# Attention output of a transformer block on one core: heads' sums through DRAM without transposes, divided as rows

## The reference

```
Q, K, V = heads(x @ Wq), heads(x @ Wk), heads(x @ Wv)      # (b, head, s, 8)
weights = softmax(mask(Q K^T / sqrt(8)))
attn = (weights @ V).reshape(b, s, 128)                    # no transpose back
x = layernorm(x + attn @ Wo + bo)
```

## Time and profile before

| | |
|---|---|
| Median of 3 runs | 1116.17 us (1111.87 to 1117.45) |
| Profiled execution: time, span | 1118.13 us, 1116.4 us |
| Mean granted clock of PE, share of full | 0.964 |
| Busy: PE, DVE, POOL, ACT | 87%, 74%, 61%, 60% |
| One period of the attention loop | 43.8 us |

### The profile page before, as it was taken

How to read it: one execution, slowest core, us unless ns; L and a number is a source line. 1 busy time by engine, 2 the same in 40 slices (tenths; PEclk the granted TensorE clock), 3 DMA queues, 4 the chain that set the end, 5 groups by cost and what they waited for, 6 DMA issues and landing times.

```text
span 1116.4 us, 29852 instructions
## 1 busy us (share of the span) xinstructions
PE 966.8 (87%) x9185; PEld 640.2 (57%) x9185; DVE 830.4 (74%) x2262; ACT 665.9 (60%) x1338; POOL 683.8 (61%) x1063
## 2 busy tenths in 40 slices
PE   3789999999999989999999999879899889998750
PEld 1344454454545545544455455349899879997740
DVE  4777878888888898898888888974455455467744
ACT  1256657666666676676666766646475745556552
POOL 7022445775766766756657667666668546557874
PEclk9699999999999999999999999979899999999985
DMA  7523133143242342432432423343222223265515
GB/s 168 186 74 115 57 96 121 50 138 102 65 137 91 87 128 64 121 122 51 138 101 66 134 74 98 117 139 89 71 73 71 78 67 87 71 200 183 166 54 169
DMA packets 134569, 117.75 MB, mean 105 GB/s; under 512 B 56218, under 2 KB 99777, under 8 KB 134240
## 3 DMA queue, kind: packets, MB, share of 16 engines
q1 hardware_dynamic: 121808, 96.37, 29.7%
q0 software_dynamic: 8704, 17.06, 4.5%
q10 hardware_dynamic: 3904, 2.43, 0.9%
HBM read 65.26 MB, written 53.81 MB: 107 GB/s over the span
## 4 chain that ended last, share of the span: by engine, by line
PE 43%; DVE 18%; POOL 11%; issue 10%; ACT 7%; DMA 6%; SPq 4%; ACTq 1%; DVEq 0%; POOLq 0%
PE ring L1132 9%; PE ring L1148 9%; DVE negmax L1192 8%; PE ps_v L1072 5%; PE ring L1009 4%; PE ring L1040 4%; ACT probs L730 3%; POOL probs L598 2%; PE ring L1055 2%; SPq L397 2%; POOL rows_d L610 2%; PE ps_m L937 2%; POOL y_d L640 2%; DMA rows<-att_d 2%; PE ps_m L902 2%
## 5 line engine op out<-in xcount | busy, mean ns | idle before, releaser
L730 ACT ACTIVATE probs<-ring 128x768 f32<-128x768 f32 (+1 forms) x384 | 337.3, 883 | 213.5 <-PE ring L1009 212.5
L1192 DVE TENSOR_REDUCE negmax<-ring 128x2 f32<-128x1024 f32 (+3 forms) x512 | 409.3, 812 | 67.5 <-PE ring L1055 63.8
L598 POOL TENSOR_SCALAR_AFFINE_SELECT probs<-probs 128x512 f32<-128x512 f32 x256 | 163.6, 639 | 247.5 <-ACT probs L730 245.4
L840 ACT ACTIVATE vpad<-ring,b_s 128x128 f32<-128x128 f32 x576 | 165.0, 371 | 107.8 <-PE ring L1132 105.9
L640 POOL DMA_INDIRECT y_d<-vpad,xs x144 | 146.1, 1015 | 102.3 <-DVE vpad L1496 75.4
L1009 PE MATMUL ring<-qarea,kside 64*128 64x512 f32 (+3 forms) x1024 | 178.6, 387 | 24.0 <-DVE negmax L1192 18.0
L1040 PE MATMUL ring<-kside,qarea 64*128 64x256 f32 (+2 forms) x1024 | 166.5, 363 | 28.8 <-ACT probs L730 15.1
L1009 PEld LDWEIGHTS ring<-qarea,kside 64*128 64x128 f32 x1024 | 87.3, 187 | 179.3 <-issue 118.8
L1072 PE MATMUL ps_v<-probs,vpad 128*32 128x512 f32 (+3 forms) x2048 | 180.4, 448 | 1.8 <-POOL probs L598 1.8
L1148 PE MATMUL ring<-qarea,vpad 128*128 x1152 | 157.5, 280 | 20.1 <-ACT vpad L840 20.0
L1132 PE MATMUL ring<-vpad,w_t 128*128 128x128 f32 x1152 | 157.1, 280 | 8.8 <-issue 8.6
(11 more groups left out here) (178 smaller groups left out, 1162.8 us busy)
## 6 DMA issues: line engine op xcount, KB each, us to landing
qk_d<-qarea SPq DMA_DIRECT2D x62, 256.0 KB, 2.6
kside<-qk_d SPq DMA_DIRECT2D x96, 128.0 KB, 3.0
qarea<-qk_d SPq DMA_DIRECT2D x90, 128.0 KB
xs<-rows_d SPq DMA_DIRECT2D x144, 66.0 KB, 1.9
probs<-y_d SPq DMA_DIRECT2D x16, 512.0 KB
xin<-L_attn_x SPq DMA_DIRECT2D x16, 256.0 KB, 3.0
att_d<-attt SPq DMA_DIRECT2D x128, 32.0 KB
rows<-att_d SPq DMA_DIRECT2D x16, 256.0 KB
```

What stands on the lines that cost most here:

```text
L598: pool.affine_select(out=diag, in_=diag, pattern=[[0, 4], [1, P]], compare_op=ALU.is_ge, fill=0.0, base=0, channel_multiplier=-1).then_inc ...
L730: nc.scalar.activation(of_unit(h // 2, part), ring[:, 2 * part % 3, :, (0, P, P)[part]:S], ACT.Exp, scale=SCALE).then_inc(sem("exp_done"), 1)
L840: ins = nc.scalar.activation(ht[:, n % 4, c, :], ps_a[:, n % 4, c * P:(c + 1) * P], ACT.Gelu_apprx_tanh, bias=b1_s[:, bass.ds(e, 1), c:c + ...
L1192: ins = nc.vector.tensor_reduce(negmax[:, n // 6 % 2, qb, s:s + 2], ring[:, (2 * n + 1) % 3, :, c0:c0 + nk], AX.X, ALU.max, negate=True)
```

## The change

The divide moves from the transposed layout to the loaded rows. ACT copies `ps_v` into `ucp`, now two halves, with the 16 rows of each group brought together by a strided write. Each half is stored at once from that layout, values and sums, by four transfers of 64 KB (in runs of 128 bytes), so eight transfers and 512 KB a block. Four loads of 128 KB (in runs of 512 bytes) bring the values as `rows16` and the sums, in the same layout, as `sums16`. DVE takes the reciprocal of all of `sums16` (128x512) at half step 21 and multiplies `rows16` by it at 22; stage wo waits for that product. The stages uT and aT, `urec`, `att` and `attt` go. The rows come in another order of channels, so Wo's rows are loaded permuted, by eight transfers instead of one, and Wq, Wk and Wv are loaded plainly, one transfer each. ACT's copy of V moves from the middle of step 4 to the start of step 5. On SP, `store_attention` of k = 1 and `load_attention` of block i - 1 now stand ahead of `store_x2`, and `store_attention` of k = 0 of block i behind it; in the tail they stand at steps 5 and 7, and `store_x2` at 6.

```
-    att_d = nc.dram_tensor("att_d", (16, HD, NH, S // 16), F32, kind="Internal").ap()
+    att_d = nc.dram_tensor("att_d", (2, 2, 2 * HD, 16, NH // 2, S // 16), F32, kind="Internal").ap()
...
-                5: ("mT", 0, 2), 6: ("uT", -1, 1), 7: ("aT", -1, 0), 9: ("mT", 0, 3), 10: ("nT", -2, 0),
-                12: ("wo", -1, 0), 13: ("mT", 1, 0), 14: ("uT", 0, 0)}
+                5: ("mT", 0, 2), 9: ("mT", 0, 3), 10: ("nT", -2, 0),
+                12: ("wo", -1, 0), 13: ("mT", 1, 0)}
...
             if i.loop or i.value < NB:
+                store_attention(sp, prev, 1)
+                load_attention(sp, prev)
                 store_x2(sp, prev.plus(-1))
-                store_attention(sp, prev)
-                load_attention(sp, prev)
+                store_attention(sp, i, 0)
...
+        def store_attention(sp, b, k):
             if not b.exists(NB):
                 return
+            need(sp, sem("u_copied"), 2, b, k + 1, sem("sp_passed"))
+            if k == 0:
+                need(sp, sem("rows16_in"), 64, b, -64, sem("sp_passed"))
+            for j in range(GH):
+                sp.dma_start(att_d[b.parity, :, :, :, GH * k + j].rearrange("a c r o -> (a c) r o"),
+                             ucp[32 * j:32 * j + 32, k].rearrange("p (r o) -> p r o", r=16)).then_inc(
+                    sem(f"att_stored{k}"), 16)
...
+            for k in range(2):
+                need(sp, sem(f"att_stored{k}"), 16 * GH, b, 16 * GH, sem("sp_passed"))
             need(sp, ready("wo"), 1, b, 0, sem("sp_passed"))
-            sp.dma_start(rows16[:, :], att_d.rearrange("r d h o -> (r d) (h o)")).then_inc(sem("rows16_in"), 16)
+            for what, t in ((0, rows16), (1, sums16)):
+                for a in range(2):
+                    sp.dma_start(t[:, :].rearrange("p (k a m) -> p a k m", k=2, a=2)[:, a],
+                                 att_d[b.parity, a, HD * what:HD * what + HD].rearrange(
+                                     "c r (k j) o -> (c r) k (j o)", k=2)).then_inc(sem("rows16_in"), 16)
...
-            load_heads(sp, wk_s, wk, "wk_in")
-            load_heads(sp, wv_s, wv, "wv_in")
-            sp.dma_start(wo_s[:], wo).then_inc(sem("weights_in"), 16)
+            sp.dma_start(wk_s[:], wk).then_inc(sem("wk_in"), 16)
+            sp.dma_start(wv_s[:], wv).then_inc(sem("wv_in"), 16)
+            for d in range(HD):
+                sp.dma_start(wo_s[16 * d:16 * d + 16, :], wo[d:D:HD, :]).then_inc(sem("weights_in"), 16)
...
-            load_heads(act, wq_s, wq, "wq_in")
+            act.dma_start(wq_s[:], wq).then_inc(sem("wq_in"), 16)
...
                 need(act, sem("pv_done"), 4, b, 2 * k + 2)
-                need(act, ready("uT"), 2, b, k)
-                nc.scalar.activation(ucp[:], ps_v[:], ACT.Copy).then_inc(sem("u_copied"), 1)
+                need(act, sem(f"att_stored{k}"), 16 * GH, b, 0)
+                nc.scalar.activation(ucp[:, k].rearrange("p (r o) -> p o r", r=16),
+                                     ps_v[:].rearrange("p (o r) -> p o r", r=16), ACT.Copy).then_inc(
+                    sem("u_copied"), 1)
...
             def st_wo(b, place):
-                need(pe, sem("rows16_in"), 16, b, 16)
+                need(pe, sem("rows_ready"), 1, b, 1)
...
+            def divide(b, part):
+                if part == 0:
+                    need(dve, sem("rows16_in"), 64, b, 64)
+                    nc.vector.reciprocal(sums16[:], sums16[:]).then_inc(sem("recip"), 1)
                 else:
+                    need(dve, sem("recip"), 1, b, 1)
+                    nc.vector.tensor_tensor(rows16[:], rows16[:], sums16[:], ALU.mult).then_inc(sem("rows_ready"), 1)
...
-                            if at == 13:
-                                divide(prev, 1, False)
-                                divide(prev, 1, True)
+                            if at in (21, 22):
+                                divide(prev, at - 21)
...
-                        if i.exists(NB) and at == 29:
-                            divide(i, 0, False)
-                            divide(i, 0, True)
```

More of the change, by code:

```diff
@@ L89, in build_program @@
     RING = 12
-    WEIGHTS = 6
+    WEIGHTS = 5 + 8
     assert (S, D, NH, QB, FC, E) == (512, 128, 16, 4, 4, 8) and NB % 2 == 0
@@ L128, in build_program @@
         xt = sb("xt", [P, S])
[L129 to L132, removed]
+        ucp = sb("ucp", [P, 2, S])
         rows16 = sb("rows16", [P, S])
+        sums16 = sb("sums16", [P, S])
         ysum = sb("ysum", [P, QB, D])
@@ L309, in place_max @@
                 sem("max_placed"), 16)
[L311 to L317, removed]
         def store_side(sp, b, side, what, hl):
@@ L487, in body @@
                     for h in range(NH):
+                        if h == 6:
+                            store_x2(sp, i.plus(-2))
                         if h == 5:
[L489 to L492, removed]
+                            store_attention(sp, i.plus(-1), 1)
+                        if h == 7:
                             load_attention(sp, i.plus(-1))
@@ L732, in body @@
                                                      ACT.Exp, scale=SCALE).then_inc(sem("exp_done"), 1)
+                        if h == 5 and u == 0 and nxt.exists(NB):
+                            copy_v(act, nxt)
                         if u != 1 and h in (0, 1) and rb.exists(NB):
@@ L816, in middle @@
                     nc.scalar.activation(rv[:, 4], rv[:, 3], ACT.Exp).then_inc(sem("gate_exp"), 1)
-                if prev.exists(NB):
-                    if h == 7:
-                        need(act, ready("aT"), 1, prev, 1)
-                        need(act, sem("att_stored"), 16 * HD, prev, 0)
-                        nc.scalar.activation(attt[:].rearrange("p (r o) -> p o r", r=16),
-                                             ps_m[:].rearrange("p (o r) -> p o r", r=16),
-                                             ACT.Copy).then_inc(freed("aT"), 1)
             def hidden(n):
@@ L883, in misc @@
                         break
-                if not i.loop and i.value >= NB and (name, i.value) in (("uT", NB), ("nT", NB + 1)):
+                if not i.loop and i.value >= NB and (name, i.value) in (("nT", NB), ("nT", NB + 1)):
                     pe.wait_ge(sem("route"), ROUTE * (i.value - 3) + 14)
@@ L910, in st_v @@
                 if not b.loop and b.value == 0:
-                    pe.wait_ge(sem("wv_in"), 16 * 4)
+                    pe.wait_ge(sem("wv_in"), 16)
                 for q in range(QB):
@@ L922, in st_mT @@
                 return ins
-            def st_uT(b, k):
-                need(pe, sem("u_copied"), 2, b, k + 1)
-                return tr(lambda q: ucp[:, q * P:(q + 1) * P])
-            def st_aT(b, place):
-                need(pe, freed("uT"), 2, b, 2)
-                return tr(lambda q: att[:, q, :])
             def st_wo(b, place):
-                need(pe, sem("rows16_in"), 16, b, 16)
+                need(pe, sem("rows_ready"), 1, b, 1)
                 if not b.loop and b.value == 0:
@@ L1226, in low_part @@
                                         ALU.subtract).then_inc(freed(stage), 1)
-            def divide(b, k, second):
-                of = ps_m[:].rearrange("p (q a c) -> p q a c", q=QB, c=16)
-                if not second:
-                    need(dve, ready("uT"), 2, b, k + 1)
-                    nc.vector.reciprocal(urec[:], of[:, :, :, 8]).then_inc(sem("recip"), 1)
-                else:
-                    need(dve, sem("recip"), 2, b, k + 1)
-                    need(dve, ready("aT"), 1, b, 0)
-                    nc.vector.tensor_tensor(att[:, :, 64 * k:64 * k + 64].rearrange("p q (a d) -> p q a d", d=HD),
-                                            of[:, :, :, 0:HD], along(urec[:], HD), ALU.mult).then_inc(freed("uT"), 1)
+            def divide(b, part):
+                if part == 0:
+                    need(dve, sem("rows16_in"), 64, b, 64)
+                    nc.vector.reciprocal(sums16[:], sums16[:]).then_inc(sem("recip"), 1)
+                else:
+                    need(dve, sem("recip"), 1, b, 1)
+                    nc.vector.tensor_tensor(rows16[:], rows16[:], sums16[:], ALU.mult).then_inc(sem("rows_ready"), 1)
             def statistics(b, which, src):
```

20 lines of the change are left out of this document (5 added, 15 removed).

## The result

The changed kernel takes 1191.6 us at the median (1190.7 to 1203.2, 4 runs), the kernel before beside it 1116.8 us: a ratio of 1.070 (95% interval 1.065 to 1.074). 1142 us was forecast, 1116 to 1156 as the range: the sign was right, the loss three times as large. The profiled execution has a span of 1189.9 us, 73.5 more than before, and a mean clock of 0.920 instead of 0.964.

What follows compares the result with a forecast made beforehand. PE and DVE, both nearly full and feeding each other through the PSUM ring, were taken as the bound. +33.6 stall, -4.4, -0.8 start, -3.8 + 1 tail gave +25.6 us on 1116.2: 1142 us, range 1116 to 1156.

Steps and rivals of the forecast that it cites:

- What goes out: Work removed per block: twelve PE transposes (1.9 us), two reciprocals and two products of DVE (1.53 us), one strided ACT copy (1.09 us).
- What comes in: Work added per block: DVE reciprocal of 128x512 at 3.1 us, product at 0.69 us; strided ACT copies taken as zero.
- rival 1: The dense reciprocal is fast (0.69 us), so nothing is paid at the wo product: about 1107 us; chance 0.14.
- Steps 10 to 12, where it is paid: The new DVE work makes PE wait ahead of the product with wo: +2.4 us in each of 14 blocks, +33.6 us.
- Rival 2: The stall is partly given back, half of 33.6 us regained before step 4: 1125 us; chance 0.20.
- Steps 6 and 7: Removed divide lets L1288 slip in ahead of POOL's product: -0.4 us a block in 11 blocks; bounds 0 and 1.1.
- Step 14: Transposes and divide removed there gain zero, as PE still waits for DVE or ACT; 0.7 a block otherwise.
- SP's queue: Stores and loads of rows stay hidden: rows in at 461.7 to 466.1, against 466.07 when DVE wants them.
- rival 3: The rows come late and the reciprocal starts up to 1.5 us later, +21 us: 1163 us; chance 0.08.
- Start and tail: Shorter wait for wk at the start -0.8 us; earlier rows in the tail -3.8, slow reciprocal +1.
- the slip: At step 6, L1288 gets in 0.12 us earlier, before POOL's product, shortening its long wait: -4.4 us over 11 blocks.

Runs made afterwards that it cites:

- e15: The kernel before, with ScalarE's two copies of the sums written strided; everything else stays: ratio 1.0004.
- e5: The kernel before, with one reciprocal of a 128x512 tile of ones added to DVE at half step 21 of each block, for which nobody waits: ratio 1.011.
- e12: The kernel before, with the four-element instruction L1288 alone moved one half step earlier: ratio 1.0037.
- e13: The changed kernel, with SP waiting for the placements of Q to land before it issues the stores of the sums of k = 1: ratio 1.079.
- e8: The kernel before, with the load of the attention rows in the tail put at step 9 instead of 11: ratio 1.0002.
- e3: The changed kernel, with twelve transposes that nothing reads put on PE just ahead of its wait for the divided rows in step 12: 1171.3 us, ratio 1.050.
- e2: The changed kernel, with three groups of four transposes of other data put back on PE at steps 6, 7 and 14: 1202.1 us, ratio 1.074.

## Why the prediction was wrong

- **What goes out** held in its prices and brought almost nothing: of the 1.2 us by which PE is earlier at step 8, 0.6 became the wait for Q in the block shown, and a second half at the full clock is only 0.2 us shorter (21.08 for 21.30).
- **What comes in.** The reciprocal took 3.34 us, 6.2 ns an element by the forecast's own fixed part, where 3.1 and 5.8 were forecast: right in kind, rival 1 is out. The Trainium skill's repeat count of 8 (VectorE: DVE Perf Modes, "First, the fixed hardware budget") made an estimated 4.4 us, which the trace does not bear out. Product 0.68 for 0.69, strided copies 1.07 for 1.09, at no cost (e15).
- **Steps 10 to 12, where it is paid** is the step that failed, by what it left out. The direct stall was forecast at 2.4 us and measured 2.3. But the step ended with PE taking up its work at full speed. In 12 of 14 blocks the clock fell to half between 0.3 us before and 2.8 us after the end of the wait, and stayed there for 3 to 10 us. That cost 31 us in the first halves; another 12 went with the half clock of the second, whose cause is open. No term, bound or rival held this. The earlier trace rows showed a clock of 1.00 and no idle of such length on PE. Yet the kernel before has such a half too, at 158 us: PE waits 0.87 us for the rows' DMA in it, and with 3.4 us at half clock it lasts 24.9 us, where the two beside it last 22.1 and 22.9.
- **Rival 2** went the wrong way: nothing was given back. e5 shows when DVE's time is partly absorbed (0.9 of 3.3 us paid): when PE does not stand waiting for its end.
- **Steps 6 and 7.** The -4.4 us were not earned. L1268, the former L1288, starts a little earlier against POOL's mask and product, ahead of both, and is still held to the product's end (L667, 499.59 + 1.27). DVE, then POOL, in one iteration of after:

```profile
498.85 2.05 DVE L1268 TENSOR_SCALAR rv<-rv 128x4 f32<-128x4 f32 x1
```

```profile
498.99 0.64 POOL L599 TENSOR_SCALAR_AFFINE_SELECT probs<-probs 128x512 f32<-128x512 f32 x1
499.59 1.27 POOL L667 TENSOR_TENSOR xc<-xc,gam_b 128x512 f32<-128x512 f32 x1
```

  e12 shows that even all of it would have brought nothing: the term was mis-sized in its bounds as well.
- **Step 14** and **SP's queue** held; rival 3 is out, but 2 to 3 us later would have been too late in five blocks (e13).
- **Start and tail.** The first K product starts at 5.85 instead of 6.56 us (0.7 of 0.8). From the last copy of the sums (at 824.5, before at 747.0) to the end of the span 365.4 us pass instead of 369.4: -4.0. The -2.8 that was summed had +1 for the last attention block in it; that block alone lost 6.5 us. e8 leaves open what part of the -4.0 is the earlier load.

With the missing 44 us of clock and without the 4.4 of the slip, the forecast's sum of 25.6 would have been 74. That it meets the 73.5 is partly luck: the stall was summed some 2 to 5 us too high, the last block some 6 too low.

## What to carry to other kernels

A wait put in front of the matrix engine in a loop that keeps it 94% busy is not priced by its length: look at the granted clock behind waits that the kernel already has, and add the time at half clock times what a microsecond of it costs in that loop (0.40 here). Work taken off an engine counts only if the next thing it waits for is not due at the same point, and a long instruction of the engine that feeds it costs least in parts, in steps where nobody stands waiting for its end (1.016 against 1.070).

## What was unexpected in the hardware

- Twelve PE transposes added in a wait made the kernel 20 us faster (e3).
- PE's clock fell behind the wait in 12 of 14 blocks of the changed kernel. There the wait was 2.28 to 3.15 us; in the two others it was 1.69 (the half from 509.76) and 2.24 us. Length alone does not decide: e2 has a fall behind 1.49 us, and e3 falls in four of 14 blocks behind the same 0.73 us.
- DVE's reciprocal of data in SBUF costs 6.2 ns an element at 512 elements (3343 ns) and 6.0 at 64 (540 ns), where a product takes 1.0, each without its fixed 0.155 us.
- A four-element instruction of DVE that met POOL's product took 1.98 us, and moved out of its way 0.17 us, without any effect on the time.
